# A graph kernel's second diffusion step: turned rows copied ahead of the third coarse level, upper and lower sums added in one PSUM bank, GpSimd's additions left out

## The reference, cut down

```python
S = S + jnp.eye(n)
Rf = S / jnp.clip(S.sum(axis=1, keepdims=True), 1e-12)
Rb = S / jnp.clip(S.sum(axis=0), 1e-12)[:, None]
Xf, Xb, Xa = (X, X, X)
for s in range(2):
    A = _adj_from_feats(Xa, W1, W2, W3)   # softmax of Q W2 K^T, cut to the top 90% of each row's mass
    Xf = Rf @ Xf
    Xb = Rb @ Xb
    Xa = A @ Xa
    Z = Z + (Xf @ U1[s] + Xb @ U2[s] + Xa @ U3[s])
```

## Time and profile before

| what | value |
|---|---|
| median of 3 runs | 2398.31 us (2397.7 to 2399.26) |
| profiled execution: span | 2397.4 us |
| PE busy | 1968.8 us, 82% |
| DVE busy | 1946.8 us, 81% |
| ACT busy | 1708.7 us, 71% |
| POOL busy | 873.0 us, 36% |
| mean granted TensorE clock | 0.932 |

### The profile page before, as it was taken

The page is one execution under the profiler, slowest core; times in us unless marked ns, Lnnn a source line. Parts: engine busy times, 40 slices in busy tenths (PEclk is TensorE's granted clock), DMA queues, the critical chain, the costliest instruction groups (busy, mean ns, idle before and its releaser), DMA issues. The chain is left out here.

```text
span 2397.4 us, 33017 instructions
## 1 busy us (share of the span) xinstructions
PE 1968.8 (82%) x10002; PEld 1296.6 (54%) x10002; DVE 1946.8 (81%) x6082; ACT 1708.7 (71%) x1806; POOL 873.0 (36%) x1438
## 2 busy tenths in 40 slices
PE   2999753999999999999945979798888888888883
PEld 1555322666666666666623555565655556555552
DVE  6777657788888888888647888988888888898885
ACT  4443236888888888888437888888887888888840
POOL 2000042344444444444433353443435344343423
PEclk9999876999999999999977999999898999999996
DMA  6777221011111111111160001001010100101023
GB/s 229 280 282 289 95 97 36 28 50 50 50 50 48 50 50 46 39 43 50 41 228 18 21 21 40 21 21 41 21 40 21 41 21 21 41 21 40 20 70 125
DMA packets 65726, 167.62 MB, mean 70 GB/s; under 512 B 7037, under 2 KB 45307, under 8 KB 61947
## 3 DMA queue, kind: packets, MB, share of 16 engines
q1 hardware_dynamic: 65530, 165.43, 19.9%
HBM read 117.95 MB, written 47.45 MB: 69 GB/s over the span
## 5 line engine op out<-in xcount | busy, mean ns | idle before, releaser
L1352 PE MATMUL banks<-xa,pt 128*128 128x256 f32 x2704 | 683.3, 407 | 126.0 <-ACT pt L920 125.9
L1352 PEld LDWEIGHTS banks<-xa,pt 128*128 128x128 f32 x2704 | 533.4, 203 | 283.3 <-ACT pt L920 139.6
L896 ACT ACTIVATE junk_a<-pb_all,minus_t 128x3327 f16<-128x3327 f32 x151 | 463.9, 3072 | 150.1 <-POOLq L823 147.5
L901 ACT ACTIVATE junk_a<-pb_all,minus_t 128x3327 f16<-128x3327 f32 x151 | 463.3, 3068 | 2.6
L1398 PE MATMUL banks<-region,at 128*128 128x512 f16 x2028 | 450.4, 381 | 0.0
L808 POOL TENSOR_SCALAR over<-over,points 128x1 f32<-128x1 f32 x151 | 164.7, 1091 | 740.5 <-ACT junk_a L901 740.4
L1398 PEld LDWEIGHTS banks<-region,at 128*128 128x128 f16 x2028 | 199.5, 98 | 231.1 <-issue 6.0
L1206 DVE TENSOR_SCALAR_CACHE_REDUCE pb_all<-banks 128x1024 f32<-128x1024 f32 x260 | 210.9, 849 | 96.6 <-PE banks L1317 93.8
L1317 PE MATMUL banks<-keys,qs 64*128 64x512 f32 (+1 forms) x832 | 199.8, 576 | 90.8 <-DVE pb_all L1206 50.2
L1344 PE MATMUL banks<-ident,pb_all 128*128 128x128 f32 x1352 | 191.7, 291 | 54.5 <-DVE pb_all L1137 34.4
L1075 DVE MAX8 junk_v<-below 128x8 f32<-128x208 f32 (+1 forms) x624 | 222.5, 432 | 2.2
(11 more groups left out here) (222 smaller groups left out, 2914.1 us busy)
## 6 DMA issues: line engine op xcount, KB each, us to landing
at<-adjT_d SPq DMA_DIRECT2D x52, 832.0 KB, 4.9
region<-in_adj_dram SPq DMA_DIRECT2D x25, 1663.5 KB, 7.9
adjT_d<-at SPq DMA_DIRECT2D x26, 832.0 KB, 3.9
fb_d<-fb_sb SPq DMA_DIRECT2D x26, 256.0 KB, 2.0
region<-fb_d SPq DMA_DIRECT2D x2, 3328.0 KB, 18.1
y_d<-y_sb SPq DMA_DIRECT2D x50, 128.0 KB, 1.9
x_d<-pb_all SPq DMA_DIRECT2D x1, 3328.0 KB, 10.4
qs<-q_d SPq DMA_DIRECT2D x104, 32.0 KB, 4.2
```

Source lines behind the costliest of these rows:

```text
L896: nc.scalar.activation(junk_a[:, 0:w], pb[u][:, 0:w], ACT.Relu, scale=sign, bias=t, accum_out=over[u][:, 0:1])\
L901: nc.scalar.activation(junk_a[:, 0:w], pb[u][:, 0:w], ACT.Sign, scale=sign, bias=t, accum_out=over[u][:, 1:2])\
L1352: last = nc.tensor.matmul(bank[4][:, 0:D], pt[sl][:, t * P:(t + 1) * P], xa[:, t0 + t, :], start=(t0 + t == 0), stop=(t0 + t == T - 1))
```

## The change

Four things change, all in the step with s = 1, save that the layout of `fb_sb` is written in step 0 for it to read:

1. The stored features are ordered as upper Xf, upper Xb, lower Xf, lower Xb, and all 52 matmuls of L1398 add into bank 5. Bank 5 then holds Xf in one half and Xb in the other. Bank 6 isn't used.
2. ACT copies two results of 128 x 256 out of it, straight into `xf_sb` and `xb_sb`, where it copied four into `t_hi` and `t256`. PE waits for these copies of the tile before, by `xfb`, where it waited by `sx_lo`.
3. POOL's two additions of 128 x 256 (`spread`) are gone.
4. Passes 4 and 5 of a tile, the third coarse level, leave the end of body i; they come in the next body behind chunk 1 of the turned rows, and passes 6 and 7 move from behind chunk 1 to behind chunk 2.

```diff
@@ -693,11 +693,6 @@
-        def sums_copied(i):
-
-            return 2 * (i.use + 1) if first else T + 4 * (i.use_here + 1)
-
-        t_hi = fb_sb[:, :].bitcast(f32).rearrange("p (n d) -> p n d", d=D)
...
@@ -773,13 +768,6 @@
-                def spread(i):
-
-                    pool.wait_ge(S2("sx_lo")[i.slot], sums_copied(i))
-                    after(pool, "fbT_psum", i + -1)
-                    for n, dst in enumerate((xf_sb, xb_sb)):
-                        nc.gpsimd.tensor_tensor(dst[i.slot][:, :], t_hi[:, n, :], t256[i.slot][:, n, :], ALU.add).then_inc(S2("xfb")[i.slot], 1)
-
@@ -829,8 +817,6 @@
-                    if not first and k.inside(T):
-                        spread(k)
@@ -847,10 +833,10 @@
-                        ch.link(nc.gpsimd.tensor_copy(fb_sb[:, 2 * D:3 * D], xk_sb[:, :]))
-                        nc.gpsimd.tensor_tensor(fb_sb[:, D:2 * D], xf_sb[k.slot][:, :], fb_sb[:, 0:D], ALU.subtract)\
+                        ch.link(nc.gpsimd.tensor_copy(fb_sb[:, D:2 * D], xk_sb[:, :]))
+                        nc.gpsimd.tensor_tensor(fb_sb[:, 2 * D:3 * D], xf_sb[k.slot][:, :], fb_sb[:, 0:D], ALU.subtract)\
                             .then_inc(S2("fb_lo")[k.slot], 1)
-                        nc.gpsimd.tensor_tensor(fb_sb[:, 3 * D:4 * D], xk_sb[:, :], fb_sb[:, 2 * D:3 * D], ALU.subtract)\
+                        nc.gpsimd.tensor_tensor(fb_sb[:, 3 * D:4 * D], xk_sb[:, :], fb_sb[:, D:2 * D], ALU.subtract)\
                             .then_inc(S2("fb_lo")[k.slot], 1)
@@ -866,7 +852,7 @@
-                STEPS = ((), (0,), (1,), (2, 3), (4,), (5,)) if first else ((), (6, 7), (), (8, 9), (), (11,))
+                STEPS = ((), (0,), (1,), (2, 3), (4,), (5,)) if first else ((), (4, 5), (6, 7), (8, 9), (), (11,))
@@ -970,18 +956,9 @@
-                            act.wait_ge(S2("xfb")[1 - i.slot], 2 * (i + 1).use)
-                            for n, sc in enumerate((rinv_s, cinv_r)):
-                                nc.scalar.activation(t_hi[:, n, :], bank[5 + n][:, 0:D], ACT.Copy, scale=sc[:, i.t, :])\
-                                    .then_inc(S2("sx_lo")[i.slot], 1)
-                                nc.scalar.activation(t256[i.slot][:, n, :], bank[5 + n][:, D:2 * D], ACT.Copy, scale=sc[:, i.t, :])\
-                                    .then_inc(S2("sx_lo")[i.slot], 1)
-                                if n == 0 and m.inside(T):
-                                    for q in range(4, 6):
-                                        sums(m, q)
-                    elif not first and m.inside(T):
-                        for q in range(4, 6):
-                            sums(m, q)
+                            for n, (dst, sc) in enumerate(((xf_sb, rinv_s), (xb_sb, cinv_r))):
+                                nc.scalar.activation(dst[i.slot][:, :], bank[5][:, n * D:(n + 1) * D], ACT.Copy, scale=sc[:, i.t, :])\
+                                    .then_inc(S2("xfb")[i.slot], 1)
@@ -1388,14 +1365,13 @@
-                        if first:
-                            pe.wait_ge(S2("xfb")[1 - i.slot], 2 * (i + 1).use)
-                        else:
-                            pe.wait_ge(S2("sx_lo")[1 - i.slot], sums_copied(i + -1))
-                        for n in range(1 if first else 2):
+                        pe.wait_ge(S2("xfb")[1 - i.slot], 2 * (i + 1).use)
+                        PARTS = 1 if first else 2
+                        for n in range(PARTS):
                             for t in range(T):
                                 mov = parts[:, t, :] if first else parts_fb[:, t, n * 2 * D:(n + 1) * 2 * D]
-                                last = nc.tensor.matmul(bank[5 + n][:, :], at[i.slot][:, t, :], mov, start=(t == 0), stop=(t == T - 1))
+                                last = nc.tensor.matmul(bank[5][:, :], at[i.slot][:, t, :], mov, start=(n == 0 and t == 0),
+                                                        stop=(n == PARTS - 1 and t == T - 1))
```

## The result

The median fell from 2398.01 to 2332.72 us (4 runs each): the ratio is 0.9724, with a 95% interval of 0.971 to 0.9738. That is 65.3 us less, where 71 were forecast. The profiled execution has a span of 2331.6 us.

A forecast was written before the change was run, and what follows sets the result against it. Bound: a loop of waits, PE for turned rows behind ACT's list, 42.09 us a cycle. New cycle 38.75 + 0.25 = 39.0; 22 x (42.09 - 39.0) + 2.8 = 71 us gained, 2398.3 - 71 = 2327; range 2318 to 2355.

The forecast's parts named there:

- The loop and its release: ACT's list delays turned rows, PE and logits; copying them earlier removes DVE's waits for logits, 3.06 us a cycle.
- T0: Moment when DVE's subtraction ends in a tile's cycle: L1137 before the change, L1114 after.
- The next loop: L1061, POOL, passes 6 to 9, `xo_sb`, its transposes, 52 matmuls, flag, L1137: 38.75 us, untouched by the change.
- the floor: Shortest cycle the change could reach, 38.75 us, read from the one cycle with no logits to make.
- PE's clock: New idle time before the large product may start it at the lower clock: bounds 0 and 1.5 us, 0.25 taken.
- the first tile: Its cycle goes by the same loop: L1137 at 1332.1 instead of 1334.87, 2.8 us gained.
- signs of being wrong: Pass 6 after T0 + 8.5; L1398 above 11.4; DVE's flag wait above 1 us at lower clock; period 42.
- The rival of the clock: Large product starts at the lower clock in most cycles: cycle 40.25, gain 43, time 2355 us; chance 0.16.
- PE's idle time: PE works from T0 + 2 to about 10, waits for the fourth copy until 15.3, then 1.8 us for `xo_sb`.
- The bound by PE's old 13.7 us: Even with the old 13.7 us from product 0 to logits 1, PE is there at T0 + 15.8.
- POOL's additions: Removing them spares DVE collisions at L1070 and L1072: between 0 and 0.94 us a cycle, 0.25 taken.
- The gap that POOL must not miss: POOL's five operations must end before L1070 at T0 + 8.37; missing: 2375 us (0.08), or every cycle 2417 (0.05).

The follow-up runs named there:

- Experiment 5: Changed kernel with POOL's addition of z to y and the one on `at` moved behind the first full level (level 3): 2336.4 us.
- Experiment 2: Changed kernel with the order undone: `STEPS` as before, passes 4 and 5 back between the two copies: 2393.6 us.
- experiments 1: Kernel before with only the order changed; four copies, two banks and POOL's two additions stay: 2333.2 us.
- 8: Kernel before with only the order changed, plus the transposes of `xo_sb` between the halves of the large product: 2317.8 us.
- experiment 7: Changed kernel with the third coarse level one place later, behind the third copy of the turned rows, directly ahead of passes 6 and 7: 2455.6 us.

## Why the prediction was right, and where a size was off

**The loop and its release: shown.** The two copies of the turned rows went from T0 + 5.1 to T0 + 1.1 and DVE's waits for logits went. The order alone gave 2333.2 us, the rest alone 2393.6.

**The next loop: shown.** The cycle without logits was taken for the floor, 38.75. With PE's clock held up, all 22 cycles are 38.74. DVE's own length is only 0.1 us below this, as the forecast had it (38.8, level with the floor), so the filler alone can't tell the two apart. Experiment 5 can: with DVE 0.63 us shorter, the cycle that no long product touches is still 38.72. Cutting the loop at `xo_sb` leads to DVE's length, with its wait of 0.66 us for POOL: 38.66. Pass 6, the fourth copy and `xo_sb` stayed where they were forecast, and the first tile's L1114 came at 1332.11 for 1332.1.

**"It is a floor": too strong.** It holds only if POOL's last level is held behind the subtraction. The cycle that follows a long product is 38.0. POOL's rows at the ends of two cycles:

```profile
1528.41 0.27 POOL L796 TENSOR_SCALAR over<-over,points 128x1 f32<-128x1 f32 x1 [5.56 <-ACT junk_a L887]
1528.78 0.27 POOL L802 TENSOR_SCALAR points<-over 128x1 f32<-128x1 f32 x1
...
1568.11 3.02 POOL L796 TENSOR_SCALAR over<-over,points 128x1 f32<-128x1 f32 x1 [5.56 <-ACT junk_a L887]
1571.23 0.26 POOL L802 TENSOR_SCALAR points<-over 128x1 f32<-128x1 f32 x1
```

In the first, the long product had put L1114 off to 1529.38; pass 11 was done 1 us earlier, and POOL ended its level 5 (L796, L802) before L1114 started. In the second, L1114 started at 1567.39, L796 came 0.7 us later and was held for 3.02 us. DVE's next search starts 0.7 us earlier in the one than in the other. So a long product gives back 0.7 of its 1.7 us in the cycle behind it: 40.4 + 38.0 = 78.4, where two undisturbed cycles are 77.5. The 0.46 us between 39.21 and 38.75 are half of that 0.9.

**PE's clock: the term that was mis-sized.** I took 0.25 us a cycle from bounds of 0 and 1.5. It was 1.68 us in every second cycle, less what the loop gave back, 0.46 a cycle; 22 x 0.21 = 4.6 us of the 5.7 by which the forecast missed. Two of my signs of being wrong came true with it: L1398 longer than 11.4, and a wait for the flag above 1 us at the lower clock. I had gone by the one cycle of the earlier trace rows, whose product stayed short behind a wait of 1.92 us; that was one draw. Experiment 2 has the same wait of 1.92 us and a product of 13.07, whose first 3 us had a clock of 0.54. The filler shows that the idle time ahead of the product is needed for it, and what it costs: 11 us. The rival of the clock (40.25 in most cycles) came half true. The Trainium skill's rule (TensorE: Matmul & The Clock Gate, What's actually happening), that recent activity sets the gate, agrees with the filler run, in which all 22 products took 11.39 us. It doesn't tell the long cycles from the short ones, ahead of which PE was idle for the same 2.13 us.

**PE's idle time was misread on the way.** I had PE at work until T0 + 10 and idle until 15.3. I took a row of 14 passes for two products; it is one, 3.29 us. PE works on to T0 + 14 and waits 1.32 us. The bound by PE's old 13.7 us held, so the sum didn't suffer.

**POOL's additions: 0.30 of the 0.94 us, as taken (0.25).** The addition of z to y took over the collision with L1047, as forecast, and the one on `at` was held behind it where the second removed addition had been. DVE's time is level with the floor, as forecast, and the saving is hidden in the changed kernel (experiments 1, 5 and 8).

**The gap that POOL must not miss** was no danger in the changed kernel, and experiment 7 shows its price: pass 6 starts 5.5 us later in each cycle.

**Outside the cycles**, the one without logits went from 38.75 to 41.07, with a large product of 13.52 us, and the one behind it from 34.55 to 33.12. I had counted nothing for either; together they cost 0.9 us more of the 5.7.

## What to carry to other kernels

When a wait is taken out, look for a cycle in the old trace that happens to lack it: its length told the new period to 0.01 us, once PE's clock was out of the way. Compare it with the length of each engine's own work too: with the order alone DVE's 38.95 us was the longer of the two. And one such cycle says nothing of what varies from cycle to cycle, as the clock does. An edit that only reorders one engine's list can hold the whole gain of a bigger change; run it alone. Ask of every new idle time on PE what runs right behind it: 2.1 us of waiting cost 1.7 us more in the product behind, in every second cycle, and either filler work or other work moved into the gap takes it back.

## What the runs showed of the hardware that was not expected

The large product alternated strictly between 13.07 and 11.39 us in the changed kernel, behind a wait of 2.13 us (once 2.37). With the order alone the wait was 1.81 us in all 22 cycles, and nine products took 12.77 to 13.07 us, the others 11.39. In experiment 5 the wait was 2.55 us, and still half of the products took 11.39. With nine filler matmuls (2.10 us) in the gap none of the 22 was long, and none in experiment 7, whose waits were below 0.9 us. Why the same idle time ends one way in one cycle and the other way in the next was not settled.

A delay on one engine can pay part of itself back: 1.7 us on PE let POOL finish ahead of a DVE instruction of 3.6 us that holds it out, and shortened the next cycle by 0.7 us.
